# GpSimd waits for ScalarE's copy of the turned rows, in place of TensorE's turn, before it refills a gather buffer

## What is computed

```python
def _cgconv(x, src, dst, attr, Wf, bf, Ws, bs):
    z = jnp.concatenate([x[dst], x[src], attr], axis=-1)
    m = jax.nn.sigmoid(z @ Wf + bf) * jax.nn.softplus(z @ Ws + bs)
    agg = jax.ops.segment_sum(m, dst, num_segments=N)
    return agg + x
...
h = _leaky_relu(_graph_norm(_cgconv(x, ...), ...))
h = _leaky_relu(_graph_norm(_cgconv(h, ...), ...))
x = _layernorm(x + h)
...
# third layer: cosine similarity of W x at both ends of an edge, weighted rows summed by source
```

## Time and profile before

| | us |
|---|---|
| median of three runs | 10861.23 (10859.53 to 10882.57) |
| the profiled execution | 10817.65 |
| its span, from the first to the last instruction | 10815.9 |
| first convolution loop, first gather to last copy | 476 to 2685 |
| second convolution loop, the same | 3004 to 5340 |
| before the first, between, after the second | 476, 319, 5476 |
| PE, DVE, ACT, POOL busy over the span | 4597.3, 4365.3, 2253.9, 7725.3 |

### The profile page before, as it was taken

How to read it: one execution, slowest core, us unless ns; L and a number is a source line. 1 busy time by engine, 2 the same in 40 slices (tenths; PEclk the granted TensorE clock), 3 DMA queues, 4 the chain that set the end, 5 groups by cost and what they waited for, 6 DMA issues and landing times. The chain is left out here.

```text
span 10815.9 us, 78044 instructions
## 1 busy us (share of the span) xinstructions
PE 4597.3 (43%) x15982; PEld 2924.7 (27%) x15982; DVE 4365.3 (40%) x7068; ACT 2253.9 (21%) x3460; POOL 7725.3 (71%) x6875
## 2 busy tenths in 40 slices
PE   0077777777057777777522222222222222222221
PEld 0033333333023333333312222222222222222221
DVE  3444344434323333333344444444444444444445
ACT  0033333434023333333311001001001000010010
POOL 5666666665666666666557888888888888888884
PEclk9978877878577777777755555555555555555555
DMA  8233333333223333333202322233233233322323
GB/s 299 74 92 93 93 93 94 97 94 91 77 75 91 88 87 92 85 92 89 71 27 43 37 36 36 35 37 37 35 37 37 35 37 37 35 36 35 37 37 72
DMA packets 720256, 736.86 MB, mean 68 GB/s; under 512 B 384442, under 2 KB 472394, under 8 KB 718890
## 3 DMA queue, kind: packets, MB, share of 16 engines
q0 software_dynamic: 398432, 244.82, 18.2%
q1 hardware_dynamic: 312520, 426.93, 12.5%
q10 hardware_dynamic: 9218, 64.36, 1.5%
HBM read 494.10 MB, written 241.38 MB: 68 GB/s over the span
## 5 line engine op out<-in xcount | busy, mean ns | idle before, releaser
L651 POOL DMA_INDIRECT by_src<-arena,put_idx x1568 | 2492.9, 1590 | 482.8 <-issue 473.3
L578 POOL DMA_INDIRECT G<-h_rows,src_idx x1568 | 1547.2, 987 | 763.1 <-issue 462.4
L578 POOL DMA_INDIRECT G<-in_x,src_idx x1470 | 1450.3, 987 | 742.9 <-issue 474.9
L756 PE MATMUL ps_gv<-ident,arena 128*128 128x128 f32 x1568 | 385.8, 427 | 3742.1 <-issue 2719.0
L578 POOL DMA_INDIRECT G<-wh_rows,src_idx x1568 | 1537.1, 980 | 478.1 <-issue 441.2
L756 PEld LDWEIGHTS ps_gv<-ident,arena 128*128 128x128 f32 x1568 | 307.5, 224 | 3803.5 <-issue 2914.7
L1033 DVE TENSOR_TENSOR_SCAN xd_t<-same,xd_t,ps_inj 128x512 f32<-128x512 bf16 x588 | 750.1, 1276 | 859.3 <-remote 652.3
L708 PE MATMUL ps_gv<-attr,w_attr 65*128 65x512 f32 x1568 | 1016.2, 784 | 0.0
L711 PE MATMUL ps_gv<-arena,w_src 128*128 128x512 f32 x1568 | 1000.9, 774 | 0.0
L1175 DVE TENSOR_SCALAR put_idx<-arena,drop 128x8 int32<-128x8 f32 x196 | 45.5, 232 | 2287.4 <-DMA by_src<-arena,put_idx 2287.3
L690 PE MATMUL ps_inj<-ident,inj 128*128 128x128 f32 x2352 | 442.6, 321 | 899.9 <-DMA inj<-first_edge_rows 652.8
(11 more groups left out here) (162 smaller groups left out, 7061.1 us busy)
## 6 DMA issues: line engine op xcount, KB each, us to landing
inj<-first_edge_rows SPq DMA_DIRECT2D x588, 256.0 KB
running_sums<-arena SPq DMA_DIRECT2D x392, 256.0 KB
same<-same_dst SPq DMA_DIRECT2D x1176, 64.0 KB
first_edge_rows<-zeros ACTq DMA_DIRECT2D x56, 896.0 KB
attr<-in_attr_t SPq DMA_DIRECT2D x392, 128.0 KB
G<-h_rows,src_idx POOLq DMA_INDIRECT x1568
G<-wh_rows,src_idx POOLq DMA_INDIRECT x1568
by_src<-arena,put_idx POOLq DMA_INDIRECT x1568
```

The lines of the kernel that those rows point to most:

```text
L578: pool.indirect_dma_start(out_, None, table_in, bass.IndirectOffsetOnAxis(ap=index, axis=0)).then_inc(s, 16)
L651: pool.indirect_dma_start(acc_d[a], bass.IndirectOffsetOnAxis(ap=put_idx[:, g % 2, k:k + 1], axis=0), put[:, g % 2, k * D:(k + 1) * D], No ...
L756: mm = pe.transpose(spread[:, buf % 2, k], src_f[:, buf % 2, k:k + 1].to_broadcast([P, P]), ident[:])
```

## The change

One wait of GpSimd is on another semaphore. In the two convolution loops (`layer < 2`), GpSimd waited for the count of `s_gt` that says that group g-4 has been turned by TensorE. It now waits for the same count of `s_xs`, which says that ScalarE has copied the turned rows of group g-4. The third loop is untouched. No instruction is added or removed, and each engine's stream stands in the same order.

```diff
@@ -631,7 +631,7 @@
                 def gather_group(g, first=0, to=SLOTS):
                     h, buf = g // NB, g % NB
                     if first == 0:
-                        wait(s_gt if layer < 2 else s_used, done(layer if layer < 2 else 0, h, buf, NB))
+                        wait(s_xs if layer < 2 else s_used, done(layer if layer < 2 else 0, h, buf, NB))
                     for k in range(first, to):
```

## The result

| | before | after |
|---|---|---|
| median of four runs each, us | 10870.61 (10859.53 to 10882.57) | 11202.87 (11175.28 to 11211.33) |
| the profiled execution, us | 10817.65 | 11175.28 |

The ratio is 1.0302, with a 95% interval of 1.0289 to 1.0314: 332 us slower, where 212 were forecast and 11175 was the upper end of the range. The direction and the place were right, the size was not. Between the two profiled executions the difference is 358 us.

The account below looks back on a forecast made before the run. GpSimd's gather stream plus its waits was taken to bound the two convolution loops. Waits rising from 322 to 409 and 305 to 430 us add 212 to 10817.65; with 44 for the median, the forecast was 11070 us, range 10855 to 11175.

Parts of the forecast that it names:

- What bounds the loops: Two convolution loops: GpSimd's stream plus real waits, nothing else; 196 x 9.62 + 322 and 196 x 10.36 + 305 us.
- Where a first gather stands after a wait: GpSimd in both loops: nearly every first gather after a wait comes 0.77 us after the end of copy L815.
- The number of waits: GpSimd's waits in the two loops become fewer: 83 and 84 in place of 90 and 93.
- What the pause gives back: Both loops: other engines run free in the added pause, so 1.35 and 1.84 us gain 0.18 and 0.22 group a cycle.
- the sum made from it: Waits of both loops: 409 us in place of 322 and 430 in place of 305, together +212 us.
- a credit of 80 us: Both loops: fewer waits through longer cycles lower the added cost from 292 to 212 us.
- The delay of one wait: GpSimd's resumption: copy's end plus 0.77 us minus today's first gather; 1.35 and 1.84 us a wait, 121 and 171 in all.
- the short kind: Waits where ScalarE stands ready for the turn: delay 0.6 us, 58 and 60 waits in the two loops.
- the long kind: Waits where ScalarE first copies the sums and does four activations: delay 4.3 us, 17 and 30 waits in the loops.
- no credit: Rival for both loops: wait counts stay at 90 and 93, delays add 292 us, giving 11153 us; chance 0.28.
- Faster: Rival for both loops: GpSimd resumes with one more group freed, long runs become the rule, 10724 us; chance 0.14.
- second rival: Both loops: pause is a need per group, so waits get rarer as they get longer; same time, 10861 us; chance 0.11.

Follow-up runs that it names:

- before_again: The kernel before, unedited, run and traced again on a chip where the kernel before takes 10860.05 us: 10861.81 us.
- after_again: The changed kernel, unedited, run and traced on the same chip as before_again: 11209.35 us, 1.0326 of the kernel before.
- short_pause_2_b: Kernel before, with GpSimd waiting after every second group for all but its last gather to land, where the kernel before takes 10168.91 us: 10456.36 us, 1.0279.
- before_3: The kernel before, unedited, traced on a chip where the kernel before takes 10168.91 us: 10169.89 us.
- drain_group: Kernel before, with GpSimd also waiting after every group of the two convolution loops until that group's own gathers have landed: 11155.95 us, 1.0328.

## Why the prediction was right in kind and wrong in size

- **What bounds the loops.** This was right. The loops are GpSimd's stream and its waits, and little else: the gathers took the same time, and the loops grew about by the waits (175 and 202 us against 161 and 208).
- **Where a first gather stands after a wait.** This was right: at the median 0.80 us after the end of L815 in both loops (the forecast said 0.77), which is what the new wait must give.
- **The number of waits.** This was right: 83 and 84 were forecast, 86 and 84 measured, so that a cycle holds 2.28 and 2.33 groups.
- **The step that failed** is "What the pause gives back", and the sum made from it. It took it that a cycle with more groups has the same mean delay, and multiplied the new number of waits by the old mean, 83 x (3.58 + 1.35) and 84 x (3.28 + 1.84), as if the mix of kinds stayed. The measured means are 5.62 and 6.11 us, not 4.93 and 5.12. The kind of a wait goes with the length of the run before it, in both kernels: after 2 groups it was short in 194 of 200 cases, after 3 groups long in 90 of 100 (in the traces of before_again and after_again in 216 of 219 and 82 of 90). So a cycle that gains a group becomes, most often, a cycle of 3 and pays the long wait at its end. Runs of 3 went from 22 and 17 to 28 and 33, and the long waits from 23 and 33 to 28 and 39.
- **What the gain was worth.** In the changed kernel's first loop the third group costs 9.62 us of gathers and 9.0 - 3.9 = 5.1 us of wait, 14.7 us, where a cycle of 2 costs 9.62 + 3.88/2 = 11.6 us a group. In the kernel before a third group cost 9.62 + 4.7 - 3.3 = 11.0, a little less than the 11.3 of a cycle of 2. So what the sum booked as a credit of 80 us (292 - 212) was none. The table gives its size: with the number and the mix of waits of before and the means of after, the two loops would have 976 us of waits; they have 996. The change of rhythm cost some 20 us in this trace, and 100 of the 157 us by which the forecast waits (409 + 430) fell short come from this step. For before_again and after_again the same working gives a cost of some 140 us.
- **The delay of one wait.** For the short kind it was right: this grew by 0.65 us in both loops. For the long kind 4.3 was forecast and 4.61 and 4.99 came; the results themselves arrived later after the last gather, 3.64 and 3.75 us on average in place of 2.89 and 2.88. There were also more waits of this kind in the trace of before than the 17 and 30 that the sum took at 4.3. This too-small term makes up the other 57 us. It is also the main reason why the measured 332 lies above the 292 of "no credit".
- **The rivals.** None of them let the mix change, and none could reach the measured time. The data was at hand: the long kind and the run of 3 could have been counted together in the trace of before, where 34 of 39 runs of 3 ended long.
- **The evidence between the rivals.** The comparison by length of pause (2.30 and 1.93 groups after long ones, 2.27 and 2.22 after middling ones) was read as speaking for "no credit". It counts groups, and says nothing on what a longer cycle costs.
- **"Faster".** This rival fell: 3 groups to a cycle would have broken even only with waits of 4.93 us, and at the end of 3 groups the long wait is 9.
- **The condition.** The prediction took the holding back as a property of the kernel. It did not occur on every chip. Where it is absent the second rival's "same time" is the result, for another reason than that rival's: GpSimd never waits for this semaphore. One trace could not tell that.

That the mix of kinds, and not the delay alone, makes the size is read from the traces of two pairs of runs. No experiment held the rhythm fixed while it changed the delay.

## What to carry to other kernels

A wait that is moved to a later event costs what the releasing engine has queued ahead of that event, and it can be long: here 0.6 us when ScalarE stood ready and 4.4 when it had four activations first. When such a delay changes the rhythm, don't multiply a new count by an old mean; sort the waits by what precedes them and ask which kind the new cycles will have. And free a buffer at its last reader: the copy never read this buffer, and the later release bought nothing on any chip on which the two kernels were compared.

## What the runs showed of the hardware

- The same kernel before took 10796 to 10871 us (medians) on four occasions and 10146 and 10169 on two others, on other chips. On the first kind of chip, results of TensorE reach the other engines many microseconds late while GpSimd issues indirect DMAs in a row (products recorded until 1508.49 are followed at 1524.14). Of the products whose recorded end fell in the 12th gather after a wait or later, none of 168 reached VectorE within 0.5 us in the kernel before and none of 205 in the changed one; of the earlier ones 131 of 224 and 148 of 187 did. On the second kind of chip nothing of this shows in the traces.
- What makes the difference between the chips, and what carries the delay, stays open. No chip is on record for two occasions, so that chip and occasion are not told apart. Nor does any run separate the number of gathers from time, since a spacing between gathers was not tried.
- The holding back ends after GpSimd stops: the awaited result comes 2.5 to 2.9 us after its last gather's end after a run of 2 groups (the short kind), and 3.5 to 3.9 us after 3 (the long kind; medians of each loop). A pause until all own gathers have landed, 2.70 us after every 7 or 8 gathers, prevented it. One until all but the last have landed, after 15 or 16 gathers, did not (1.1 and 1.6 us on average in the loops of short_pause_2_b, where nothing else held GpSimd), nor did a full one after every 12.
- SyncE shows something on the same chips: from the first gather of the first loop to the last copy of the second, 1,404 of its 7,071 instructions took over 0.6 us in the kernel before (median 0.046), 3 of 7,071 in before_3. drain_group, where no result is late, still has 420.
